# Experts' rows turned by transposing DMAs instead of by TensorE, in a transformer block with a mixture of experts

## Chip, cores, metric

The kernel runs on one core of a Trainium2 chip. The metric is the device time of the whole program in microseconds (us), the median of several runs. Engines: TensorE (PE: matrix products and, in this kernel, transposes), VectorE (DVE), ScalarE (ACT), GpSimd (POOL), and SyncE (SP), which issues most of the DMAs. An instruction waits on semaphores, and each engine works through its own instructions in order.

## What is computed

One block over 4096 tokens of width 256: attention with 16 heads, residual and layer norm, then a mixture of 8 experts of which each token uses two, residual and layer norm. The part that matters here is the mixture:

```
probs = softmax(x @ Wg);  topv, topi = top_k(probs, 2)
pos   = position of the token among those of its expert;  keep = pos < cap      # cap = 1076
buf[expert * cap + pos] = x                                                      # each kept token, twice
h = gelu(buf[e] @ W1[e] + b1[e])          # 1076 x 256 by 256 x 1024, for each of 8 experts
y = h @ W2[e] + b2[e]                     # 1076 x 1024 by 1024 x 256
out[token] += gate * keep * y[slot of token]
x = layernorm(x + out)
```

## The kernel before

**Stages.** Attention fills the first 780 us or so, with the router of the earlier token blocks woven in. Then the router's last block runs (class `Last`), then the eight experts one after the other (function `experts`), then the last layer norm (class `Combine`). The change touches the experts.

**Where the rows come from.** The router's GpSimd scatters write each kept token as a row of 260 floats (1040 bytes) into `slots_x` in memory, row `expert * 1076 + position`. The first 1024 bytes are the token's 256 values as bf16, high part, and 256 as bf16, low part. The last four floats are tags, from which VectorE makes the token's number (`entry`) and gate (`weight`).

**Tiles of an expert.** `CAP` is 1076 rows, `ST` = 9 tiles of 128 rows, the last with `LAST` = 52. `SB` = [(0, 3), (3, 6), (6, 9)] groups the tiles into three sub-blocks of 384, 384 and 308 columns. `HC` = 8 is the hidden width in units of 128. Everything that an expert loads has two buffers, `u` = 0 and 1, so expert e + 1 is prepared during expert e.

**Loads.** SP's `load(u, e)` (L2338 to L2342) reads the rows with tags into `xe` in three DMAs: tiles 0 to 2 (semaphore `x_first`), tiles 3 to 7 and tile 8 (`x_loaded`). Before the loop it waits, in `last.sync`, for all the router's scatters, then issues `load(0, 0)` and `load(1, 1)`. In the loop it waits (L2351 to L2353) until expert e's weights are split, its rows transposed (`x_mm`) and its entries made, and then issues the weights of e + 2 (two DMAs of 1024 KB) and `load(u, e + 2)`. These waits end shortly after expert e has begun.

**Turning the rows.** The first product needs tokens along the free axis, with the 256 input values across partitions. TensorE's `transpose` (L2404) makes four 128x128 bf16 transposes of a tile into PSUM (`ps_x`). ScalarE's `tokens` (L2474) copies them into `xs`. For expert 0, tiles 0 to 2 are turned before its first product and tiles 3 to 8 between its first products. For each later expert e + 1, tile k is turned right before tile k of expert e's `down`.

**Order on TensorE, per expert** (function `one`): 8 `up` products of sub-block 0 and 8 of sub-block 1 (L2416, each six matmuls, hidden chunk q = 0 to 15), `down` of tiles 0 to 2 (L2435, 24 matmuls a tile), 8 `up` of sub-block 2 (q = 16 to 23), `down` of tiles 3 to 5 and 6 to 8. An `up` of chunk q needs ScalarE to be done with chunk q - 4 (PSUM `ps_h` has 4 buffers). `down` of tile k needs VectorE to have read tile k - 2 (`y_sum`, `ps_y` has 2 buffers).

**Order on ScalarE**: gelu of each chunk (L2483, `hidden`), which needs VectorE to be done with chunk q - 4 of `hid`; behind q = 5 and q = 13 the next expert's `W1` and `W2` are rounded to bf16 (L2263, `weights_high`); behind q = 15 the copies `tokens` of tiles 0 to 2, behind q = 23 those of tiles 3 to 8.

**Order on VectorE**: `entries` (the tags, L2559 to L2567), then `split` of chunks 0 to 15 (two operations, L2535 and L2537), then `out` of tiles 0 and 1, `split` of chunks 16 to 23, `out` of tiles 2 to 8. An `out` adds the bias out of PSUM into `yb` (L2521, after which TensorE may reuse that buffer) and multiplies by the gate into `y` (L2526). `y` has three buffers, so `y` of tile k waits until the scatter of tile k - 3 has landed (`y_stored`).

**Order on GpSimd**: the low part of the next `W1` (`w1s`, L2269), the scatters of tiles 0 to 2 (L2372, adding rows of `y` into `result`), the low part of the next `W2` (`w2s`), the scatters of tiles 3 to 8.

## Time and profile before

| | |
|---|---|
| runs, median (lowest to highest) | 1235.44 us (1235.28 to 1236.4), 3 runs |
| profiled execution, span | 1233.1 us; 2.3 us of the median lie outside the span |
| busy in the span | PE 94%, ACT 74%, DVE 52%, POOL 29% |
| experts | from 820.62 (first `up`) to 1197.45 (last `down`), 376.8 us |
| one expert | 47.2 us for those that prepare the next one, 44.4 us for the last |
| last layer norm and stores | from 1197.45 to 1233.1 |

A row of the timeline gives start and duration in us, the engine (PE matmuls, PEld weight loads that overlap them, SPq what SP's queue issues), the line of the program, the operation with output and inputs, a count, and in square brackets how long the engine had been idle and what ended that. Times are from the start of the span. DMA shares are of 16 engines.

### The profile page before, as it was taken

What the parts mean: (1) busy time and instruction counts of PE and PEld (TensorE: products, weight loads), DVE (VectorE), ACT (ScalarE), POOL (GpSimd) and SP (SyncE); (2) the same over time, 40 slices, a digit from 0 to 9 for tenths busy, and PEclk for the clock granted to TensorE, in tenths of its full rate; (3) what the DMA queues carried; (4) which work ended last, traced back from release to release, by engine and by line L of the source; (5) the groups of instructions that cost most, each with busy time, mean ns of one, the idle gap of its engine ahead of it and who ended that gap; (6) DMA issues with size and microseconds to landing.
All of it is one profiled execution on the core that took longest, in us unless ns stands there. A gap on an engine that the chain in (4) does not pass through costs nothing. (4 is left out here: it accounts for less than half of the span.)

```text
span 1233.1 us, 24778 instructions
## 1 busy us (share of the span) xinstructions
PE 1160.2 (94%) x8880; PEld 511.0 (41%) x8880; DVE 635.4 (52%) x1802; ACT 907.5 (74%) x1181; POOL 352.1 (29%) x391
## 2 busy tenths in 40 slices
PE   9999999999999999999999989699999999999980
PEld 4332222222222222222222111277777787787770
DVE  5644343132366345724353203548767767767747
ACT  3889999999999999999999989344434435435314
POOL 5521111111123112232222220033453453552440
PEclk9999999999999999999999999799999999999995
DMA  6842421332321331214120101543443523430226
GB/s 186 178 112 79 96 66 61 80 89 73 80 77 51 112 87 45 78 55 106 40 78 27 47 14 26 180 139 86 115 72 84 129 30 106 124 34 11 28 23 272
DMA packets 84099, 104.10 MB, mean 84 GB/s; under 512 B 15415, under 2 KB 69308, under 8 KB 83984
## 3 DMA queue, kind: packets, MB, share of 16 engines
q1 hardware_dynamic: 66520, 76.80, 21.9%
q0 software_dynamic: 15968, 24.12, 9.3%
q10 hardware_dynamic: 1496, 1.68, 0.4%
q8 instruction: 68, 1.11, 0.4%
q14 instruction: 47, 0.39, 0.1%
HBM read 56.88 MB, written 47.96 MB: 85 GB/s over the span
## 5 line engine op out<-in xcount | busy, mean ns | idle before, releaser
L1497 ACT ACTIVATE prob<-ps_s 128x1024 f32<-128x1024 f32 (+4 forms) x841 | 709.1, 1006 | 41.8 <-PE ps_s L1380 39.0
L1397 PE MATMUL ps_o<-prob,v_aug 128*17 128x512 f32 (+3 forms) x3236 | 420.3, 568 | 3.0 <-DVE acc L1581 2.3
L1380 PE MATMUL ps_s<-qop,kop 51*128 51x512 f16 (+3 forms) x1618 | 273.1, 370 | 14.9 <-issue 3.9
L1380 PEld LDWEIGHTS ps_s<-qop,kop 51*128 51x128 f16 x1618 | 66.0, 93 | 399.3 <-ACT prob L1497 358.1
L2435 PE MATMUL ps_y<-w2s,hs 128*128 128x256 bf16 (+1 forms) x1728 | 189.1, 273 | 0.6 <-DVE yb L2521 0.6
L2483 ACT ACTIVATE hid<-ps_h,b 128x384 f32<-128x384 f32 (+1 forms) x192 | 105.1, 560 | 108.6 <-PE ps_h L2416 80.8
L2416 PE MATMUL ps_h<-xs,w1s 128*128 128x384 bf16 (+1 forms) x1152 | 179.9, 315 | 5.2 <-ACT hid L2483 4.5
L1581 DVE COPY acc<-ps_o 32x512 f32<-32x512 f32 (+2 forms) x108 | 74.2, 687 | 205.9 <-PE ps_o L1397 204.3
L2435 PEld LDWEIGHTS ps_y<-w2s,hs 128*128 128x128 bf16 (+1 forms) x1728 | 157.7, 99 | 17.5 <-DVE yb L2521 0.7
L2372 POOL DMA_INDIRECT result<-y,entry x72 | 111.6, 1550 | 175.5 <-DVE y L2526 140.6
L1533 POOL TENSOR_SCALAR_AFFINE_SELECT prob<-prob 128x256 f32<-128x256 f32 (+1 forms) x179 | 68.7, 395 | 310.3 <-ACT prob L1497 308.6
L2416 PEld LDWEIGHTS ps_h<-xs,w1s 128*128 128x128 bf16 x1152 | 111.2, 98 | 68.8 <-ACT hid L2483 7.2
L2040 POOL DMA_INDIRECT slots_x<-xsplit,dest_all x64 | 64.0, 1000 | 252.2 <-ACT prob L1497 195.9
L2474 ACT ACTIVATE xs<-ps_x 128x512 bf16<-128x512 bf16 (+1 forms) x72 | 40.0, 570 | 103.8 <-PE ps_x L2404 103.7
L1397 PEld LDWEIGHTS ps_o<-prob,v_aug 128*17 128x17 f32 x3236 | 58.5, 95 | 129.2 <-issue 81.4
L2535 DVE CAST hs<-hid 128x384 bf16<-128x384 f32 (+1 forms) x192 | 92.0, 479 | 38.6 <-ACT hid L2483 38.1
L2537 DVE TENSOR_TENSOR hs<-hid,hs 128x384 bf16<-128x384 f32 (+1 forms) x192 | 102.2, 532 | 6.6
L2526 DVE TENSOR_SCALAR y<-yb,weight 128x256 f32<-128x256 f32 (+1 forms) x72 | 45.7, 635 | 13.1 <-DMA result<-y,entry 8.5
L829 DVE CAST x_all<-ps_r 128x256 f16<-128x256 f32 x24 | 10.2, 424 | 76.6 <-PE ps_r L680 76.6
L2521 DVE TENSOR_TENSOR yb<-ps_y,b 128x256 f32<-128x256 f32 x64 | 27.0, 422 | 43.5 <-PE ps_y L2435 43.1
L2269 POOL TENSOR_TENSOR w1s<-w,w1s 128x2048 bf16<-128x2048 f32 x7 | 28.6, 4083 | 44.5 <-ACT w1s L2263 26.4
L1907 DVE TENSOR_TENSOR slogit<-ps_r,xg 128x8 f32<-128x8 f32 x28 | 4.7, 167 | 68.9 <-PE ps_r L1871 68.9
(206 smaller groups left out, 796.8 us busy)
## 6 DMA issues: line engine op xcount, KB each, us to landing
w<-in_W SPq DMA_DIRECT2D x16, 1024.0 KB, 7.5
slots_x<-empty POOLq DMA_DIRECT2D x12, 520.0 KB, 3.9
qop<-fparts_q SPq DMA_DIRECT2D x42, 128.0 KB, 4.7
xe<-slots_x SPq DMA_DIRECT2D x8, 650.0 KB
aT<-attnT SPq DMA_DIRECT2D x16, 256.0 KB
x_all<-in_x SPq DMA_DIRECT2D x8, 512.0 KB
result<-x_all SPq DMA_DIRECT2D x8, 512.0 KB
x_all<-result SPq DMA_DIRECT2D x8, 512.0 KB, 6.5
```

Source lines behind the costliest of these rows:

```text
L1380: mm = pe.matmul(ps_s[:, u.p % SLOTS_S, e, a.q0:], o.key(e, a.h, a.kt), o.query(e, a.h, a.b, a.q0), start=True, stop=True)
L1397: mm = pe.matmul(ps_o[32 * c:32 * c + VW, a.q0:], o.v[:, a.kt, a.h], prob[:, t % RING, c % 2, c // 2, a.q0:], start=a.first, stop=a.last)
L1497: act.activation(prob[:, t % RING, n, e:z, q0:], ps_s[:, u.p % SLOTS_S, e:z, q0:], ACT.Exp, scale=1.0 / (SCALE * SCALE)).then_inc(exp_done, 1)
L1533: pool.affine_select(own, own, [[0, z - e], [1, P]], ALU.is_ge, 0.0, base=0, channel_multiplier=-1).then_inc(masked, 1)
L1581: dve.tensor_copy(acc[rows, a], ps_o[rows]).then_inc(evicted, 1)
L2040: pool.indirect_dma_start(out=r.slots_x, out_offset=bass.IndirectOffsetOnAxis(ap=r.dest_all[:, n, m:m + 1], axis=0), in_=r.xsplit[:, m // ...
L2372: pool.indirect_dma_start(out=result, out_offset=bass.IndirectOffsetOnAxis(ap=entry[0:n, u, k:k + 1], axis=0), in_=y[0:n, k % 3], in_offse ...
L2416: mm = pe.matmul(ps_h[:, q % 4, 0:w], w1s[:, u, i1, c, m * P:(m + 1) * P], xs[:, u, i2, c, a:a + w], start=(t == 0 and c == 0), stop=(t == ...
L2435: mm = pe.matmul(ps_y[to:to + n, (ST * u + k) % 2, 0:D], hs[:, (3 * u + sbk) % 2, i1, m, o:o + n], w2s[:, u, i2, m, :], start=(t == 0 and ...
L2483: act.activation(hid[:, q % 4, 0:w], ps_h[:, q % 4, 0:w], ACT.Gelu_apprx_tanh, bias=b1[:, e, q % HC:q % HC + 1]).then_inc(gelu, 1)
L2535: dve.tensor_copy(hs[:, sl, 0, q % HC, 0:w], hid[:, q % 4, 0:w]).then_inc(h_high, 1)
L2537: dve.tensor_tensor(hs[:, sl, 1, q % HC, 0:w], hid[:, q % 4, 0:w], hs[:, sl, 0, q % HC, 0:w], ALU.subtract).then_inc(h_low, 1)
```

## The change

The rows are no longer loaded as they lie. `sync` issues, per expert, two DMAs that transpose on their way from `slots_x` into `xs`: rows 0 to 383 and rows 384 to 1087 (`TURNED`; 1076 is rounded up to a multiple of 16, the twelve rows more are never used). Two more DMAs bring the tags alone, 16 bytes a row, into `tags`. `xe`, `ps_x`, TensorE's `transpose`, ScalarE's `tokens` and their semaphores are gone. TensorE waits for the first part before sub-block 0 of `up` and for the second before sub-block 1. ScalarE runs its 24 chunks without a break. As the DMA now writes `xs` itself, SP's loop waits until all of expert e's `up` products are done (`h_mm`) where it waited for its transposes, and only then issues the weights and rows of e + 2. VectorE's entries wait for the tags.

```diff
--- before.py
+++ after.py
@@ -2223,6 +2223,7 @@
 
 
 SB = [(0, 3), (3, 6), (6, ST)]
+TURNED = [(0, 3 * P), (3 * P, -(-CAP // 16) * 16)]
 
 
 class Experts:
@@ -2274,7 +2275,7 @@
     w1s, w2s, b1, b2, ident, ws, ye_mm = X.w1s, X.w2s, X.b1, X.b2, X.ident, X.ws, X.ye_mm
     with ExitStack() as st:
         warm = sb("warm5", [1, 1], F32)
-        xe = sb("xe", [P, 2, ST, ROW], F32)
+        tags = sb("tags5", [P, 2, ST, ROW - D], F32)
         same = sb("same", [P, ST], F32)
         pick = sb("pick", [P, ST], F32)
         weight = sb("weight", [P, 2, ST], F32)
@@ -2287,12 +2288,9 @@
         y_other = sb("y_other", [HALF, D], F32)
         ps_h = psum("ps_h", [P, 4, QB], F32, st)
         ps_y = psum("ps_y5", [P, 2, QB], F32, st)
-        ps_x = psum("ps_x", [P, 2, 2 * QB], BF16, st)
-
-        x_first = [sem(f"xe_first{u}") for u in range(2)]
-        x_loaded = [sem(f"xe_loaded{u}") for u in range(2)]
-        x_mm = sem("x_mm")
-        x_out = sem("x_out")
+
+        x_turned = [[sem(f"x_turned{u}{k}") for k in range(len(TURNED))] for u in range(2)]
+        tags_loaded = [sem(f"tags_loaded{u}") for u in range(2)]
         h_mm = sem("h_mm")
         gelu = sem("gelu")
         h_high = sem("h_high")
@@ -2305,7 +2303,6 @@
         y_stored = [sem(f"y_stored{k}") for k in range(3)]
 
 
-        nc.sync.sem_inc(x_out, 2)
         nc.sync.sem_inc(h_low, 4)
         nc.sync.sem_inc(ye_mm, 2 * ST)
         nc.sync.sem_inc(h_mm, 2 * 24)
@@ -2331,15 +2328,18 @@
             for u in range(2):
                 one(E - 2 + u, E // 2 - 1, u, u == 0)
 
-        xs_d = slots_x[0:SLOTS].rearrange("(e r) d -> e r d", e=E)
+        rows_d = slots_x.bitcast(BF16)
         with nc.Block() as block:
             @block.sync
             def _(sp):
                 def load(u, e):
-                    z = SB[0][1]
-                    sp.dma_start(xe[:, u, 0:z], xs_d[e, 0:z * P].rearrange("(k p) d -> p k d", p=P)).then_inc(x_first[u], 16)
-                    sp.dma_start(xe[:, u, z:ST - 1], xs_d[e, z * P:(ST - 1) * P].rearrange("(k p) d -> p k d", p=P)).then_inc(x_loaded[u], 16)
-                    sp.dma_start(xe[0:LAST, u, ST - 1], xs_d[e, (ST - 1) * P:CAP]).then_inc(x_loaded[u], 16)
+                    for k, (a, z) in enumerate(TURNED):
+                        sp.dma_start_transpose(xs[:, u, :, :, a:z].rearrange("p a c n -> p (a c) n"),
+                                               rows_d[bass.ds(e * CAP + a, z - a), 0:2 * D]).then_inc(x_turned[u][k], 16)
+                    z = (ST - 1) * P
+                    sp.dma_start(tags[:, u, 0:ST - 1], slots_x[bass.ds(e * CAP, z), D:].rearrange("(k p) d -> p k d", p=P)
+                                 ).then_inc(tags_loaded[u], 16)
+                    sp.dma_start(tags[0:LAST, u, ST - 1], slots_x[bass.ds(e * CAP + z, LAST), D:]).then_inc(tags_loaded[u], 16)
 
                 last.sync(sp, X, io)
                 load(0, 0)
@@ -2348,7 +2348,7 @@
                     for u in range(2):
                         e = 2 * i + u
                         sp.wait_ge(ws, e * 2 + 2)
-                        sp.wait_ge(x_mm, e * ST + ST)
+                        sp.wait_ge(h_mm, e * 24 + 24 + 48)
                         sp.wait_ge(entry_done, e * 4 + 4)
                         X.load_weights(sp, io, u, e + 2)
                         load(u, e + 2)
@@ -2390,20 +2390,6 @@
             def _(pe):
                 last.tensor(pe, ps_h, ps_y[:, 0], ps_y[:, 1])
                 pe.wait_ge(X.const, 16 * (E + 3))
-
-                def transpose(e, i, u, k):
-                    if k == 0:
-                        pe.wait_ge(x_first[u], i * 16 + 16)
-                    if k == SB[0][1]:
-                        pe.wait_ge(x_loaded[u], i * 32 + 32)
-                    pe.wait_ge(x_out, e * ST + (k + 1))
-                    alone(pe)
-                    n = rows_of(k)
-                    rows = xe[0:n, u, k, 0:D].bitcast(BF16)
-                    for c in range(4):
-                        mm = pe.transpose(ps_x[:, (ST * u + k) % 2, c * P:c * P + n], rows[:, c * P:(c + 1) * P],
-                                          ident[0:n, 0:n])
-                    mm.then_inc(x_mm, 1)
 
                 def up(e, u, sbk, m):
                     w = width(sbk)
@@ -2417,11 +2403,8 @@
                                            start=(t == 0 and c == 0), stop=(t == 2 and c == 1))
                     mm.then_inc(h_mm, 1)
 
-                def down(e, i, u, sbk, ahead):
+                def down(e, u, sbk):
                     for k in range(*SB[sbk]):
-                        if ahead:
-
-                            transpose(e + 1, i + u, 1 - u, k)
                         n = rows_of(k)
                         o = (k - SB[sbk][0]) * P
                         pe.wait_ge(y_sum, e * ST + (k + 1))
@@ -2438,25 +2421,18 @@
 
                 def one(e, i, u, ahead):
                     pe.wait_ge(ws, e * 2 + 2)
-                    first = isinstance(e, int) and e == 0
-
-                    pe.wait_ge(x_out, e * ST + (SB[0][1] if first else ST) + 2)
+                    pe.wait_ge(x_turned[u][0], i * 16 + 16)
                     for m in range(HC):
                         up(e, u, 0, m)
-                        if first and SB[0][1] + m < ST:
-                            transpose(0, 0, 0, SB[0][1] + m)
-                    if first:
-                        pe.wait_ge(x_out, ST + 2)
+                    pe.wait_ge(x_turned[u][1], i * 16 + 16)
                     for m in range(HC):
                         up(e, u, 1, m)
-                    down(e, i, u, 0, ahead)
+                    down(e, u, 0)
                     for m in range(HC):
                         up(e, u, 2, m)
-                    down(e, i, u, 1, ahead)
-                    down(e, i, u, 2, ahead)
-
-                for k in range(*SB[0]):
-                    transpose(0, 0, 0, k)
+                    down(e, u, 1)
+                    down(e, u, 2)
+
                 over_experts(pe, one)
 
             @block.scalar
@@ -2464,15 +2440,6 @@
                 last.scalar(act, X)
                 act.wait_ge(X.const, 16 * (E + 3))
                 act.activation(warm[:], b1[0:1, 0, 0:1], ACT.Gelu_apprx_tanh)
-
-                def tokens(e, u, k):
-                    act.wait_ge(x_mm, e * ST + (k + 1))
-
-                    act.wait_ge(h_mm, e * 24 + 24)
-                    n = rows_of(k)
-                    src = ps_x[:, (ST * u + k) % 2, 0:4 * P].rearrange("p (c n) -> p c n", c=4)
-                    act.activation(xs[:, u, :, :, k * P:k * P + n].rearrange("p a c n -> p (a c) n"), src[:, :, 0:n],
-                                   ACT.Identity).then_inc(x_out, 1)
 
                 def one(e, i, u, ahead):
                     def hidden(q):
@@ -2483,24 +2450,11 @@
                         act.activation(hid[:, q % 4, 0:w], ps_h[:, q % 4, 0:w], ACT.Gelu_apprx_tanh,
                                        bias=b1[:, e, q % HC:q % HC + 1]).then_inc(gelu, 1)
 
-                    first = isinstance(e, int) and e == 0
-                    for q in range(2 * HC):
+                    for q in range(3 * HC):
                         hidden(q)
-                        if first and SB[0][1] + q < ST:
-                            tokens(0, 0, SB[0][1] + q)
                         if ahead and q in (5, 13):
                             X.weights_high(act, e + 1, i + u, 1 - u, q // HC)
-                    if ahead:
-                        for k in range(*SB[0]):
-                            tokens(e + 1, 1 - u, k)
-                    for q in range(2 * HC, 3 * HC):
-                        hidden(q)
-                    if ahead:
-                        for k in range(SB[1][0], ST):
-                            tokens(e + 1, 1 - u, k)
-
-                for k in range(*SB[0]):
-                    tokens(0, 0, k)
+
                 over_experts(act, one)
                 z.scalar(act)
 
@@ -2543,8 +2497,7 @@
 
                 def entries(e, i, u):
 
-                    dve.wait_ge(x_first[u], i * 16 + 16)
-                    dve.wait_ge(x_loaded[u], i * 32 + 32)
+                    dve.wait_ge(tags_loaded[u], i * 32 + 32)
                     if not (isinstance(e, int) and e < 2):
 
                         for k in range(3):
@@ -2556,15 +2509,15 @@
                     parts = [(P, slice(0, ST - 1)), (LAST, slice(ST - 1, ST))]
                     for n, ks in parts:
                         mine = X.expert[0:n, bass.ds(e, 1), ks].rearrange("p o k -> p (o k)")
-                        dve.tensor_tensor(same[0:n, ks], xe[0:n, u, ks, D + 1], mine, ALU.is_equal).then_inc(picked, 1)
-                        dve.tensor_scalar(entry[0:n, u, ks], xe[0:n, u, ks, D], 0.5, None, ALU.mult).then_inc(entry_done, 1)
+                        dve.tensor_tensor(same[0:n, ks], tags[0:n, u, ks, 1], mine, ALU.is_equal).then_inc(picked, 1)
+                        dve.tensor_scalar(entry[0:n, u, ks], tags[0:n, u, ks, 0], 0.5, None, ALU.mult).then_inc(entry_done, 1)
                     for q, (n, ks) in enumerate(parts):
                         dve.wait_ge(picked, e * 4 + (q + 1))
-                        dve.scalar_tensor_tensor(out=pick[0:n, ks], in0=same[0:n, ks], scalar=2.0, in1=xe[0:n, u, ks, D + 3],
+                        dve.scalar_tensor_tensor(out=pick[0:n, ks], in0=same[0:n, ks], scalar=2.0, in1=tags[0:n, u, ks, 3],
                                                  op0=ALU.mult, op1=ALU.add).then_inc(picked, 1)
                     for q, (n, ks) in enumerate(parts):
                         dve.wait_ge(picked, e * 4 + (q + 3))
-                        dve.tensor_tensor(weight[0:n, u, ks], pick[0:n, ks], xe[0:n, u, ks, D + 2], ALU.min).then_inc(entry_done, 1)
+                        dve.tensor_tensor(weight[0:n, u, ks], pick[0:n, ks], tags[0:n, u, ks, 2], ALU.min).then_inc(entry_done, 1)
 
                 def one(e, i, u, ahead):
                     entries(e, i, u)
```

## Rows read from the trace of the kernel before

**Rows 1.** Busy time by stage: the fourth expert and the last.
```profile
964.17:1011.41 47.24, 46.53 (x397) 35.87 (x398) 34.29 (x76) 21.29 (x35) 22.01 (x12) 1.00 0.40 91
1153.06:1197.45 44.39, 44.37 (x361) 33.95 (x360) 28.74 (x76) 13.42 (x24) 14.20 (x10) 1.00 0.21 24
```

**Rows 2.** Chain that ended last, fourth expert: start, duration, work.
```profile
989.29 6.28 PE ps_h L2416 x48
995.57 0.22 PE ps_x L2404 x4
```

**Rows 3.** Timeline, from the router's last block to the first expert.
```profile
799.39 19.11 PE L2099 MATMUL ps_y<-aT 128*128 128x256 f32 x80
...
813.98 0.37 SPq L2340 DMA_DIRECT2D xe<-slots_x  x1
...
819.46 0.17 DVE L2559 TENSOR_TENSOR same<-xe,expert_no 128x8 f32<-128x8 f32 x1 [2.12 <-issue]
...
820.62 1.14 PE L2416 MATMUL ps_h<-xs,w1s 128*128 128x384 bf16 x6 [0.73 <-issue]
```

**Rows 4.** Loads of rows (L2340), and SP's queue from 813 to 820.
```profile
DMA to landing us min/median/max: 3.1/8.2/9.5
...
q1 hardware_dynamic: 1619, 1.62, 74.6%
```

**Rows 5.** Timeline, first expert: GpSimd's split, a cast, tiles 0 and 2.
```profile
830.68 4.08 POOL L2269 TENSOR_TENSOR w1s<-w,w1s 128x2048 bf16<-128x2048 f32 x1 [18.02 <-issue]
...
831.01 3.97 DVE L2535 CAST hs<-hid 128x384 bf16<-128x384 f32 x1 [1.55 <-ACT hid L2483]
...
843.25 0.42 DVE L2521 TENSOR_TENSOR yb<-ps_y,b 128x256 f32<-128x256 f32 x1
...
844.19 2.02 PE L2435 MATMUL ps_y<-w2s,hs 128*128 128x256 bf16 x17
```

**Rows 6.** Timeline, fourth expert: entries, yb of tile 0, tile 2 on TensorE.
```profile
966.20 0.17 DVE L2559 TENSOR_TENSOR same<-xe,expert_no 128x8 f32<-128x8 f32 x1
...
985.66 0.42 DVE L2521 TENSOR_TENSOR yb<-ps_y,b 128x256 f32<-128x256 f32 x1
...
986.28 0.39 PE L2404 MATMUL ps_x<-ident,xe 128*128 128x128 bf16 x4
...
986.50 2.78 PE L2435 MATMUL ps_y<-w2s,hs 128*128 128x256 bf16 x24
```

**Rows 7.** Waits of TensorE, fourth expert: total, times, longest.
```profile
PE ps_h L2416 <- ACT hid L2483: 0.7, 1, 0.7
```

**Rows 8.** Timeline, sixth expert: scatters and y of its later tiles.
```profile
1093.34 1.55 POOL L2372 DMA_INDIRECT result<-y,entry  x1 [7.75 <-DVE y L2526]
1093.49 0.35 DVE L2526 TENSOR_SCALAR y<-yb,weight 128x256 f32<-128x256 f32 x1
...
1099.17 1.55 POOL L2372 DMA_INDIRECT result<-y,entry  x1 [0.17 <-issue]
...
1102.88 1.55 POOL L2372 DMA_INDIRECT result<-y,entry  x1 [0.30 <-issue]
1102.92 0.35 DVE L2526 TENSOR_SCALAR y<-yb,weight 128x256 f32<-128x256 f32 x1 [0.93 <-DMA result<-y,entry]
...
1107.46 0.34 DVE L2526 TENSOR_SCALAR y<-yb,weight 52x256 f32<-52x256 f32 x1
```

**Rows 9.** Timeline, first expert: scatter 2, y of tile 3, scatter 3.
```profile
856.36 1.57 POOL L2372 DMA_INDIRECT result<-y,entry  x1 [7.90 <-DVE y L2526]
856.67 5.52 DVE L2526 TENSOR_SCALAR y<-yb,weight 128x256 f32<-128x256 f32 x1
...
863.03 1.55 POOL L2372 DMA_INDIRECT result<-y,entry  x1 [1.00 <-DVE y L2526]
```

**Rows 10.** DMA queues, 966 to 976: GpSimd's while SP's loads.
```profile
q0 software_dynamic: 262, 0.21, 17.1%
```

**Rows 11.** Busy time and granted clock after the last product.
```profile
1202.00:1204.00 2.00, 0.00 (x0) 0.00 (x0) 0.00 (x0) 0.00 (x0) 0.00 (x0) 0.50 0.14 8
```

## Prediction, made before the changed kernel ran

> **What bounds the kernel now.** Busy time by stage first: an expert that prepares the next one takes 47.24 us with TensorE busy for 46.53 of them at a granted clock of 1.00 (the third number from the right), the last one, which prepares nothing, 44.39 us [rows 1]. So TensorE sets the pace, and the 2.85 us between the two are what preparing costs it. The chain of waits then says what these are: before a tile's 24 matmuls the chain holds 0.22 us of transposes [rows 2], nine times an expert, so 2.0 us; and TensorE's waits show one of 0.7 us on ScalarE's gelu among the first products [rows 7]. Behind that wait stands VectorE: gelu needs a buffer that VectorE has split.
>
> That second finding decides the sum, so I followed VectorE through one expert, in the timeline. From its entries to `yb` of tile 0 are 19.46 us without a gap worth naming (966.20 to 985.66): 16 splits of about 0.9 and one cast that a GpSimd split beside it holds up, as the cast at 831.01 is held for 3.97 us beside the split that began at 830.68 [rows 5, 6]. TensorE's tile 2 needs that `yb`. It ends at 986.08, the transposes of tile 2 begin at 986.28: VectorE is 0.2 us ahead, no more. At the end of the expert the gate is another one: `y` of tile 8 needs scatter 5 landed. A scatter lands 3.75 us after its start (1099.17 to the `y` of tile 6 that waited for it, 1102.92), others of this kind up to 3.9; I take 3.85. Scatter 5 starts at 1102.88, lands at 1106.73, and `y` of tile 8 starts at 1107.46 [rows 8]: 0.73 to spare, call it 0.8. So a second loop runs just under TensorE's: entries, splits, tile 2, the third sub-block's splits, `y` of tile 2, scatter 2, GpSimd's split of `W2`, scatters 3 to 5, `y` of tile 8, entries. Of the 2.0 us only tile 2's transposes lie in it.
>
> **Steady state, experts 1 to 5.** TensorE alone would gain 2.0 us. In the second loop two things give way. Tile 2: without the transposes of tiles 0 and 1 TensorE would be there at 986.28 - 0.44 = 985.84, but `yb` ends at 986.08; with 0.08 for the semaphore its matmuls start at 986.16 instead of 986.50 [rows 6], 0.34 earlier. At the end, the slack of 0.8 before scatter 5 is used up. From there the loop is as long as it was: 0.34 + 0.78 = 1.12 us an expert, and TensorE's wait of 0.7 grows by the other 0.9.
>
> ScalarE's nine copies an expert go too; ScalarE is busy for 21.29 of 47.24 us [rows 1] and appears nowhere in the loop but with a gelu, so nothing follows. SP's wait moves. It ended shortly after an expert's start; now it ends with the last `up`, at 995.57 (989.29 + 6.28 [rows 2]), 31.4 us after the expert's start at 964.17. Queued behind it are 2 MB of weights, the transposing DMAs and the tags. The weights are first read by ScalarE some 8 us into the next expert (GpSimd's part follows at 830.68, 10 us after 820.62 [rows 3, 5]), so they have about 23 us; at the rate below they need 7. The turned rows are wanted 63 us after the wait ends. Both are covered; were the cover gone, each missing us would cost one.
>
> But that traffic now lies beside scatters 2 to 8, on whose landing the loop depends. While SP's queue was full, GpSimd's queue took 17.1% of 16 engines over 10 us for 262 packets, 0.10 us a packet [rows 10]; a scatter has 8 per engine. If each waits for nothing, the cost is 0; if each waits for one packet of equal length, 0.8 us. Most of the transfers should be over when scatter 5 starts, 44 us in, so I take 0.2: 0.92 us an expert, 5 x 0.92 = 4.6 us.
>
> **Expert 6 and the last.** Expert 7 has no split of weights beside it, waits for nothing, 44.37 of 44.39 us busy [rows 1], and follows TensorE. So expert 6 gives tile 2's 0.34, and its tiles 3 to 8 give 6 x 0.22 = 1.3 in full: 1.6 us. The stage behind, norm and stores, is not touched.
>
> **The start.** This is where the new operation is on the path, and no row shows one. The load was issued at 813.98 and its first 390 KB had landed 3.1 us later [rows 3, 4]. In those microseconds 1619 packets with 1.62 MB took 74.6% of 16 engines x 7 us = 83.6 us [rows 4]: 52 ns for a packet of 1 KB, 19.4 GB/s an engine, 310 GB/s in all. So 390 KB are 1.26 us of transfer and 1.8 are fixed; data flows from 815.8. A row must be cut into at least four pieces of 256 bytes, since its 512 values go to four groups of 128 partitions. Call the time of a piece on its engine t. The first part (384 rows) has 96 pieces an engine, both parts (1088 rows) 272. From below: t = 13 ns, as fast as bytes were copied. From above: t = 52 ns, a piece as dear as a whole packet of 1 KB. I take the middle, 26 ns, a rate of 157 GB/s, as pieces of a quarter of the size should lie between.
> First part: 815.8 + 2.5 = 818.3. TensorE runs its filling matmuls until 818.50 [rows 3], so it begins at 818.6, 2.0 us sooner than at 820.62, and without transposes between its products. Second part: 822.9, wanted at 826.5. Tags: 67 pieces an engine more, 1.7 us, at 824.6. That is the one that counts: VectorE's entries began at 819.46 [rows 3] and now begin at 824.6, and 19.5 us later comes `yb` of tile 0, at 844.1 instead of 843.25. TensorE's eight buffers run full meanwhile and its lead is gone; tile 2 starts at 844.1 + 0.42 + 0.08 = 844.6 instead of 844.19 [rows 5]: 0.4 us lost.
> Ends: at 13 ns the tags are there at about 819.7, VectorE is never late and TensorE's earlier start carries through, 2.5 us gained; at 52 ns they are there at 815.8 + 14.1 + 3.5 = 833.4, 9.2 us lost.
>
> Expert 0 has something of its own. Its `y` of tile 3 began 0.31 us after scatter 2 and was held for 5.52 us, so that scatter 3 began at 863.03 [rows 9]; in the sixth expert it began 0.15 us after scatter 2, took 0.35 us, and scatter 3 followed 5.83 us after scatter 2 instead of 6.67 [rows 8, 9]. Without the transposes of tile 3 `y` comes 0.22 sooner against scatter 2, on the good side: 0.84 us. Expert 0 in the loop: -0.4 + 0.84 + 0.78 = 1.2 us.
>
> **Sum.** 1.2 + 4.6 + 1.6 = 7.4 us. The profiled execution would span 1233.1 - 7.4 = 1225.7; with the 2.3 us that the median lies above the span, 1228.0.
>
> **The Trainium skill on the price of a piece.** Rows 4 give 52 ns for a plain packet and say nothing of a turned one. The skill speaks on both sides. "VectorE: DVE Perf Modes", section "The three transpose paths", gives 1309 ns for a 128x128 bf16 block by DMA and 390 ns on TensorE; its section "Rules for kernel authors" names TensorE first where PSUM will do as destination. Taken as a rate, which is an estimate of mine, that is 34 blocks x 1.309 = 44.5 us an expert; the result is the second rival below, at about 1267. "Advanced Engine Details and Errata", section "X-Bar Transpose (TRN2)", calls transposing DMAs as fast as regular ones; by that the start would be at my lower end and the time 1225. No run so far bears out either.
>
> **Rivals.**
> *Full gain.* VectorE's loop has more give than I read, and TensorE gets its 2.0 us: 7 experts x 2.0, 1.3 of expert 0's own transposes, less or more by the start (-2 to +2): about 15, so 1220. For it: TensorE is busy for all but 0.7 us. Against it: the 0.2 and 0.8 us of slack above. 0.10.
> *Slow turning (slower).* Turning costs several times a copy. Place: the start of expert 0. At t = 104 ns, what an adding packet takes in rows 10, both parts land at 815.8 + 28.3 and the tags 7 us later, at 851. TensorE then stands from 818.5 to 826 and again for the second part; after the last product the clock stood at 0.50, the 1.2 GHz level, from 1202 [rows 1, 11], so this adds a little. The entries are 26.5 us later than in my case: 1228.0 + 26.5 = 1254. It decides from the point where the 7.4 us are eaten: tags at 832, t near 47 ns, inside my bounds. Later experts stay covered, 35 us of transfer against 63. 0.22.
> *Crowded scatters.* The turning DMAs hold engines in long stretches and scatters 3 to 5 land L us later; each of seven experts pays L. At L = 1.1 nothing but the ends is left, 1233; at L = 2, 1240. For it: the loop has no slack left. Against it: the price per packet in rows 10, and transfers that should mostly be over. 0.10.
> *Forecast*, t from 13 to 47 ns: 0.58.
>
> **Range and chances.** The forecast's own range is 1224 (t = 13, no crowding: 2.9 + 1.1 less) to 1235. With full gain below and the nearer half of the slow cases above: 1221.5 to 1242; left out are most of slow turning beyond 75 ns (0.13) and the lower tail of full gain (0.04). About 0.2%, 2.5 us, is what a measurement can tell. Faster by more: the forecast but its dearest t (0.54), full gain (0.10), a little crowding (0.02), 0.66. Within: 0.09. Slower: slow turning beyond t = 55 and crowding with L over 1.5, 0.25.
>
> **What would show it.** In the new trace: the first `up` at 818.6 and the entries of expert 0 near 824.6 (time of landing, hence t); experts 1 to 5 at 46.3 us; TensorE's wait for gelu at 1.3 to 1.7 us an expert and a wait of `y` of tile 8 on the scatter; expert 7 unchanged at 44.4. I am wrong if the entries come after 832, if experts fall to 45.3 (full gain), or if scatters land more than 5 us after their start.

## Result and profile after

| | before | changed |
|---|---|---|
| median (lowest to highest) | 1235.65 us (1235.28 to 1236.4), 4 runs | 1224.26 us (1222.37 to 1226.66), 4 runs |
| ratio to before, 95% interval | | 0.9908 (0.9894 to 0.9922) |
| profiled span | 1233.1 | 1220.3 |
| first load of rows issued | 813.98 | 812.49 |
| from there to the last product | 383.5 | 372.3 |
| expert 0 | 49.2 | 45.3 |
| one expert, 1 to 5 | 47.1 to 47.3 | 45.8 to 46.8 |
| expert 6, expert 7 | 47.1, 44.4 | 45.4, 44.4 |

The changed kernel is 11.4 us faster in the median and 11.2 us faster by the stage that the change touches. 1.5 us of the 12.8 by which the two spans differ lie ahead of the first load, in code that no kernel here changes; over the thirteen profiles of this study that load is issued anywhere from 810.2 to 815.3. So what is compared below is the stage, from the first load of rows to the last product, and the median stands beside it. Of its 11.2 us, 1.5 lie between the first load and the first `up`, 3.9 in expert 0, 4.2 in experts 1 to 5 and 1.6 in expert 6. Expert 0 was longer before than the 47.2 us that the text ahead of the prediction gives for every expert that prepares the next one, since TensorE also turned six tiles of its own rows in it:

```profile
820.62:869.77 49.15, 48.12 (x420) 37.05 (x421) 34.59 (x64) 23.95 (x41) 18.77 (x9) 1.00 0.35 88
```

Busy time by stage of the changed kernel, for experts 0, 3, 6 and 7 (columns as in rows 1: PE, PEld, DVE, ACT, POOL, then granted clock, DMA share, GB/s); experts 3 and 7 answer to [rows 1]:

```profile
817.66:862.96 45.30, 44.71 (x361) 33.84 (x360) 31.14 (x69) 16.49 (x26) 17.59 (x8) 1.00 0.60 112
955.86:1002.35 46.49, 44.71 (x362) 33.84 (x360) 34.48 (x77) 16.50 (x26) 22.07 (x11) 1.00 0.47 95
1094.86:1140.30 45.44, 44.73 (x363) 33.86 (x361) 34.62 (x77) 16.49 (x26) 22.22 (x11) 1.00 0.23 26
1140.30:1184.74 44.44, 44.44 (x362) 34.01 (x360) 28.42 (x77) 13.44 (x24) 15.74 (x10) 1.00 0.22 26
```

TensorE's busy time in expert 3 fell from 46.53 to 44.71; the transposes are what is gone. The expert shortened by only 0.75, and the rest is a longer wait of TensorE for gelu, where [rows 7] has 0.7:

```profile
PE ps_h L2402 <- ACT hid L2450: 1.7, 1, 1.7
```

Expert 6, during which nothing is loaded, is at 45.44, 1.6 us shorter than before.

The start, timeline of the changed kernel (answers to [rows 3, 5]):

```profile
812.49 4.44 SPq L2337 DMA_TRANSPOSE xs<-slots_x  x2
...
817.66 13.81 PE L2402 MATMUL ps_h<-xs,w1s 128*128 128x384 bf16 x84
...
820.31 0.17 DVE L2512 TENSOR_TENSOR same<-tags,expert_no 128x8 f32<-128x8 f32 x1 [4.46 <-DMA tags<-slots_x]
...
826.38 4.07 POOL L2270 TENSOR_TENSOR w1s<-w,w1s 128x2048 bf16<-128x2048 f32 x1 [15.21 <-issue]
...
838.95 0.42 DVE L2475 TENSOR_TENSOR yb<-ps_y,b 128x256 f32<-128x256 f32 x1
```

And SP's queue from 812.5 to 820.5 (packets, MB, share of 16 engines; answers to [rows 4]):

```profile
q1 hardware_dynamic: 6270, 1.32, 84.4%
```

84.4% of 16 engines over 8 us are 108 us for 6270 packets, 17 ns each. That is a mean over unlike packets: taken apart by size, the 5093 turned pieces of 256 bytes took 19 ns each (18 in the median) and the 1076 of 16 bytes, the tags, 9 ns. The entries of expert 0 begin 7.8 us after the load is issued (820.31 - 812.49). `yb` of tile 0 comes 26.5 us after it; before it was 29.3 (843.25 - 813.98 [rows 3, 5]).

The end of expert 3, same kernel: scatters 2 to 5, and `y` of tiles 5 to 8 (answers to [rows 8]):

```profile
988.17 0.38 SPq L2256 DMA_DIRECT2D w<-in_W  x1
...
989.21 10.04 SPq L2337 DMA_TRANSPOSE xs<-slots_x  x2
...
991.06 1.55 POOL L2372 DMA_INDIRECT result<-y,entry  x1 [7.38 <-DVE y L2480]
...
996.88 1.55 POOL L2372 DMA_INDIRECT result<-y,entry  x1 [0.17 <-issue]
998.44 0.35 DVE L2480 TENSOR_SCALAR y<-yb,weight 128x256 f32<-128x256 f32 x1 [1.24 <-DMA result<-y,entry]
...
998.73 1.55 POOL L2372 DMA_INDIRECT result<-y,entry  x1 [0.31 <-issue]
...
1000.59 1.55 POOL L2372 DMA_INDIRECT result<-y,entry  x1 [0.30 <-issue]
...
1001.97 0.35 DVE L2480 TENSOR_SCALAR y<-yb,weight 128x256 f32<-128x256 f32 x1 [2.84 <-DMA result<-y,entry]
...
1003.88 0.44 DVE L2480 TENSOR_SCALAR y<-yb,weight 128x256 f32<-128x256 f32 x1 [1.22 <-DMA result<-y,entry]
...
1005.13 0.48 DVE L2473 TENSOR_TENSOR yb<-yb,y_other 52x256 f32<-52x256 f32 x1
...
1005.64 0.65 DVE L2480 TENSOR_SCALAR y<-yb,weight 52x256 f32<-52x256 f32 x1
```

A `y` that waited for its scatter dates the landing. Scatter 2 lands 7.4 us after its start (998.44 - 991.06), scatters 3 and 4 after 5.1 (1001.97 - 996.88, 1003.88 - 998.73), where [rows 8] had 3.75. `y` of tile 8 follows VectorE's own work on `yb` (1005.13 to 1005.61) without idle time, so it didn't wait for scatter 5; nor does it in experts 0 to 5 of this run. What holds VectorE up are scatters 2, 3 and 4: 1.24, 2.84 and 1.22 us. The weights are issued at 988.17, the turning DMAs from 989.21 to 999.25.

### The profile page after: what moved, and what is told of

It reads as the page before. It is cut to its first block and busy times, and to the rows that moved or that the text cites. A ratio compares the mean times of both kernels' runs of the same rounds, so it can differ in the third digit from the quotient of the medians.

```text
span 1220.3 us, 23933 instructions
## 1 busy us (share of the span) xinstructions
PE 1144.6 (94%) x8592; PEld 494.8 (41%) x8592; DVE 634.3 (52%) x1802; ACT 869.8 (71%) x1109; POOL 352.7 (29%) x391
## 5 line engine op out<-in xcount | busy, mean ns | idle before, releaser
L2418 PE MATMUL ps_y<-w2s,hs 128*128 128x256 bf16 (+1 forms) x1728 | 182.7, 273 | 0.5 <-DVE yb L2475 0.2
L2491 DVE TENSOR_TENSOR hs<-hid,hs 128x384 bf16<-128x384 f32 (+1 forms) x192 | 117.3, 611 | 6.6
L2489 DVE CAST hs<-hid 128x384 bf16<-128x384 f32 (+1 forms) x192 | 77.9, 406 | 26.9 <-ACT hid L2450 26.6
L2480 DVE TENSOR_SCALAR y<-yb,weight 128x256 f32<-128x256 f32 (+1 forms) x72 | 46.9, 651 | 37.2 <-DMA result<-y,entry 33.6
L680 PE MATMUL ps_r<-xs_half,ws_half 128*128 128x256 f16 x288 | 39.8, 274 | 0.0
```

The lines of the kernel that those rows point to most:

```text
L2418: mm = pe.matmul(ps_y[to:to + n, (ST * u + k) % 2, 0:D], hs[:, (3 * u + sbk) % 2, i1, m, o:o + n], w2s[:, u, i2, m, :], start=(t == 0 and ...
L2489: dve.tensor_copy(hs[:, sl, 0, q % HC, 0:w], hid[:, q % 4, 0:w]).then_inc(h_high, 1)
L2491: dve.tensor_tensor(hs[:, sl, 1, q % HC, 0:w], hid[:, q % 4, 0:w], hs[:, sl, 0, q % HC, 0:w], ALU.subtract).then_inc(h_low, 1)
```

## Experiments

For each, the stage from the first load to the last product, experts 1 to 5 and the median; each median has its own runs of before beside it.

| run | stage | experts 1 to 5 | expert 6 | median | ratio (95%) |
|---|---|---|---|---|---|
| before | 383.5 | 47.1 to 47.3 | 47.1 | | |
| changed | 372.3 | 46.3, 46.6, 46.5, 46.8, 45.8 | 45.4 | 1224.26 | 0.9908 (0.9894 to 0.9922) |
| moved_only | 384.2 | 47.1 to 47.3 | 47.1 | 1235.34 | 0.9993 (0.9981 to 1.0005) |
| w_early | 368.8 | 45.4 to 46.1 | 45.4 | 1219.99 | 0.9869 (0.9846 to 0.9892) |
| rows_late | 368.3 | 45.4 to 45.7 | 45.4 | 1222.65 | 0.9894 (0.9866 to 0.9923) |
| y9_after | 368.1 | 45.4 to 45.6 | 45.4 | 1217.66 | 0.9852 (0.9833 to 0.9870) |
| plain_copy | 375.5 | 47.1, 47.2, 47.1, 47.1, 45.8 | 45.8 | 1227.47 | 0.9937 (0.9919 to 0.9955) |
| tags_mid | 378.5 | 47.2, 48.2, 48.1, 48.1, 45.6 | 46.5 | 1230.79 | 0.9959 (0.9942 to 0.9975) |
| twice | 389.8 | 48.0, 50.5, 49.1, 49.2, 47.0 | 46.7 | 1242.14 | 1.0057 (1.0037 to 1.0077) |
| all_three | 368.4 | 45.4 to 45.7 | 45.4 | 1219.45 | 0.9871 (0.9853 to 0.9889) |
| tags_early | 370.5 | 45.9, 46.1, 45.7, 46.3, 45.6 | 45.5 | 1221.64 | 0.9888 (0.9866 to 0.9910) |
| copies_kept | 372.4 | 45.9, 46.5, 46.4, 46.9, 45.8 | 45.4 | 1223.23 | 0.9902 (0.9884 to 0.9919) |
| pe_kept | 392.6 | 47.1, 48.1, 53.2, 48.9, 50.4 | 47.9 | 1239.18 | 1.0026 (1.0016 to 1.0036) |

**The moved load alone** (moved_only): the kernel before, with one wait more.

```diff
                         sp.wait_ge(x_mm, e * ST + ST)
+                        sp.wait_ge(h_mm, e * 24 + 24 + 48)
                         sp.wait_ge(entry_done, e * 4 + 4)
```

> The kernel before, whose SP queue waits, as the changed kernel does, for the last up product of expert e before it issues the weights and rows of e + 2; the rows are still turned by TensorE. My theory (a loop over VectorE, GpSimd and scatters 3 to 5 with 0.8 us of slack): scatter 3 lands late beside the load, scatter 5 hardly; experts 1 to 5 between 47.2 and 47.7 us, in all 0 to 2.5 us slower than before. Rival (the moved load delays the loop strongly, and the changed kernel gains in spite of it): the y of tile 6 waits 3 to 4 us and hands on at least 1 us to each of the experts 1 to 6, 6 us or more slower in all.

VectorE waited 3.7 us in expert 3 for scatters instead of 1.4, and nothing followed: the experts have their old lengths, and the 0.7 us by which the stage is longer lie ahead of the first product. So the crowding, scatters that land late beside SP's load, is there, and the kernel before had slack for it. In the changed kernel that slack is used up.

**Away from the scatters, in two steps.** w_early takes the weights out of the way:

```diff
                         sp.wait_ge(ws, e * 2 + 2)
-                        sp.wait_ge(h_mm, e * 24 + 24 + 48)
                         sp.wait_ge(entry_done, e * 4 + 4)
                         X.load_weights(sp, io, u, e + 2)
+                        sp.wait_ge(h_mm, e * 24 + 24 + 48)
                         load(u, e + 2)
```

> The changed kernel, with the weights of e + 2 issued shortly after expert e begins, as before the change; only the transposing DMAs and the tags wait for the last up product. My theory: 1.1 MB less than 40 us into the expert, so scatter 3 lands in about 4 us instead of 7, y of tile 6 waits 1 us; each of the experts 1 to 6 gains 0.1 to 0.4 us, 1 to 2 us in all against the changed kernel. Rival (turning itself, not the weights, holds up the scatters): landing stays near 7 us and the time within 0.5 us of the changed kernel's.

rows_late is the same with `e * 24 + 24 + 48 + 1` in the lower wait.

> As the one with early weights, and the transposing DMAs wait besides for the first up product of expert e + 1, so that nothing at all lies beside the scatters 3 to 5. My theory: scatters land in 3.8 to 4 us, experts 1 to 5 at 46.1 us, 1.5 to 2.5 us faster than the changed kernel. Rival (crowding costs nothing, since only the last scatter counts): within 0.5 us of it.

Expert 3 of w_early and of rows_late, busy time by stage:

```profile
953.76:999.89 46.13, 44.72 (x363) 33.82 (x361) 34.93 (x76) 16.48 (x26) 22.06 (x11) 1.00 0.47 95
```

```profile
956.28:1001.93 45.65, 44.73 (x363) 33.85 (x361) 34.28 (x76) 16.50 (x26) 22.35 (x11) 1.00 0.49 96
```

The stage gains 3.5 and 3.9 us on the changed kernel, more than the 1 to 2 and 1.5 to 2.5 that my theory gave. With the weights gone, `y` of tile 5 no longer waits for scatter 2 in any expert, with the turning DMAs where they were; so the rival of w_early, that turning itself holds the scatters up, falls. (What the expectations of w_early and tags_early call scatter 3 is scatter 2 as counted here.) The experts of rows_late come to 45.6, not to the 46.1 at which I had put the second loop (the one over VectorE and the scatters). That loop was wrong by a term, and the timeline shows which. In my prediction VectorE has no gap from its entries to `yb` of tile 0. It has one, where gelu stands behind ScalarE's rounding of `W1`. Below, the operation that GpSimd's split holds up, in the fourth expert of before, of rows_late and of the changed kernel:

```profile
973.30 3.97 DVE L2535 CAST hs<-hid 128x384 bf16<-128x384 f32 x1 [0.88 <-ACT hid L2483]
```

```profile
965.48 3.97 DVE L2489 CAST hs<-hid 128x384 bf16<-128x384 f32 x1 [0.41 <-ACT hid L2450]
```

```profile
965.25 4.36 DVE L2491 TENSOR_TENSOR hs<-hid,hs 128x384 bf16<-128x384 f32 x1
```

There are 0.88 us of idle time before the held cast, then 0.41, then none; in the changed kernel the cast is already done, and the operation behind it is the one that is held. Entries that begin late use this gap up before they cost anything.

**No wait on the scatters of the same expert** (y9_after): nine buffers for `y`. The edit, without the two lines that follow from it (the scatter reads and VectorE writes `y[0:n, k]`):

```diff
-        y = sb("y", [P, 3, D], F32)
+        y = sb("y", [P, ST, D], F32)
-                    if not (isinstance(e, int) and e == 0 and k < 3):
-                        dve.wait_ge(y_stored[k % 3], e * (16 * ST // 3) + (k // 3) * 16)
+                    if k == 0 and not (isinstance(e, int) and e == 0):
+                        for v in range(3):
+                            dve.wait_ge(y_stored[v], e * (16 * ST // 3))
```

> The changed kernel with nine buffers of y, one for each tile, so that no y waits for a scatter of the same expert. My theory (the loop through scatter 5 holds experts 1 to 5 at 46.3 us, above TensorE's 45.4): the experts fall to 45.4 to 45.8, 3 to 5 us faster than the changed kernel, about 1220; TensorE's wait for gelu falls back to 0.5 to 0.8 an expert. Rival (VectorE's own work from entries to tile 0 sets the pace, scatters don't): experts stay at 46.2 to 46.6, within 0.5 us of the changed kernel.

```profile
951.63:997.21 45.58, 44.72 (x362) 33.84 (x361) 34.66 (x76) 16.48 (x26) 22.12 (x11) 1.00 0.47 96
```

The stage takes 368.1 us, 4.2 less, with all traffic where the change put it. TensorE's wait for gelu is back to what it was before:

```profile
PE ps_h L2402 <- ACT hid L2450: 0.7, 1, 0.7
```

So it is the wait of `y` for its scatter that hands the crowding on. The median, 1217.66, is the lowest of all, 6.6 us below the changed kernel's; by the profiles 2.3 of these are an earlier start of the stage (810.17 against 812.49), not its doing. rows_late shows the opposite: the stage is as short, but in the profile it began at 814.64, and the median is only 1.6 us lower.

**What the crowding is made of.** plain_copy brings the same 256-byte pieces without turning them. The edit in `load` (its range of rows and TensorE's four times higher waits are left out here):

```diff
-                        sp.dma_start_transpose(xs[:, u, :, :, a:z]..., rows_d[bass.ds(e * CAP + a, z - a), 0:2 * D])
+                        for c in range(4):
+                            sp.dma_start(xs[:, u, c // 2, c % 2, a:z].rearrange("p (k j) -> p k j", j=P),
+                                         rows_d[bass.ds(e * CAP + a, z - a), c * P:(c + 1) * P].rearrange("(k p) j -> p k j", p=P))
```

> The changed kernel with each transposing DMA replaced by four plain ones that bring the same rows in the same 256-byte pieces and don't turn them (output wrong: the first products see unturned rows; 1152 rows instead of 1088, 6% more). My theory (a turned piece costs about what a plain piece of 256 bytes costs): expert 0's tags land within 1 us of where the changed kernel has them, y waits for scatters as long, time within 1.5 us of it. Rival (turning is what fills the DMA engines): tags 1.5 us or more sooner, scatters land sooner, experts 1 to 4 below 46.0 us.

```profile
960.60:1007.68 47.08, 44.89 (x363) 33.76 (x361) 35.00 (x78) 16.50 (x26) 22.06 (x11) 1.00 0.48 95
```

Plain pieces crowd no less than turned ones; the stage is even 3.2 us longer than the changed kernel's, to which 6% more rows and eight DMAs in place of two may contribute. How much is theirs is open. The entries of expert 0 began 8.8 us after the load, against 7.8. So turning is not what fills the engines. My bound of 1.5 us was missed, on the side against the rival.

twice issues each turning DMA once more, first into a buffer of its own (`twice[:, u, :, a:z]`), with TensorE's waits raised to 32.

> The changed kernel with each transposing DMA issued twice, the first time into a buffer that nobody reads. My theory (17 ns a piece): the tags of expert 0 land 4.5 to 5 us later, which costs the start about 4.5 us; and 1.1 MB more beside the scatters, so that experts 1 to 4 rise from 46.5 to 47 to 48 us; about 1232. Rival (the crowding comes from the weights' 2 MB alone): the start as above, experts within 0.2 us, about 1229.

```profile
815.18 1.57 SPq L2338 DMA_TRANSPOSE twice<-slots_x  x1
...
827.89 0.17 DVE L2515 TENSOR_TENSOR same<-tags,expert_no 128x8 f32<-128x8 f32 x1 [9.36 <-DMA tags<-slots_x]
```

Entries begin 12.7 us after the load is issued instead of 7.8: 272 pieces an engine more cost 4.9 us, 18 ns each. `yb` of tile 0 comes 30.9 us after it instead of 26.5, 4.4 later; experts 1 to 5 rise to between 47.0 and 50.5. The stage is 17.5 us longer, more than twice what I had expected. Scatter 4 now lands 7.3 to 7.7 us after its start in experts 1 to 3, by the `y` of tile 7 that waited for it. About 1.7 us of expert 2's 50.5 are another thing (my estimate from the row below): for 3.4 us behind a wait of 2.1 us for gelu, the granted clock of TensorE stood at 0.50, the 1.2 GHz level.

```profile
935.30:938.60 3.30, 3.30 (x11) 1.55 (x12) 3.19 (x8) 2.46 (x5) 0.00 (x0) 0.50 0.03 7
```

tags_mid moves the two tag DMAs between the two turning ones; tags_early takes them out of `load` and issues them as soon as the entries of expert e are made:

```diff
+                        sp.wait_ge(entry_done, e * 4 + 4)
+                        load_tags(u, e + 2)
                         sp.wait_ge(ws, e * 2 + 2)
                         sp.wait_ge(h_mm, e * 24 + 24 + 48)
-                        sp.wait_ge(entry_done, e * 4 + 4)
```

> The changed kernel with the two tag DMAs issued between the first and the second transposing DMA. My theory (VectorE's entries wait for the tags at the start): entries of expert 0 begin about 5 us after the load is issued instead of 7.8, its splits wait for the first gelu only, yb of its tile 0 comes 0.8 to 1.3 us sooner after the load; experts 1 to 6 as in the changed kernel; about 1 us faster. Rival (GpSimd's split, not the tags, sets that yb): no change in it.

> The changed kernel, with the tags of e + 2 loaded as soon as expert e's entries are made, early in expert e; weights and transposing DMAs as in the changed kernel. Theory after the run with the tags in the middle (the 1076 packets of 16 bytes a load are what scatter 3 lands behind): experts 1 to 4 fall from 46.3-46.8 to 45.5-46.0 us, from the first load of rows to the last product 369 to 370 us instead of 372.3. Rival (weights and turned rows fill the engines, the tags only add a little): experts 1 to 4 stay above 46.2, 371.5 us or more.

Entries of expert 0 in tags_mid, and expert 3 of both:

```profile
814.58 1.57 SPq L2338 DMA_TRANSPOSE xs<-slots_x  x1
...
819.65 0.17 DVE L2515 TENSOR_TENSOR same<-tags,expert_no 128x8 f32<-128x8 f32 x1 [1.70 <-DMA tags<-slots_x]
```

```profile
960.48:1008.53 48.05, 45.02 (x362) 33.60 (x360) 34.57 (x76) 16.50 (x26) 22.10 (x11) 1.00 0.46 91
```

```profile
955.81:1001.55 45.74, 44.72 (x363) 33.83 (x361) 34.27 (x77) 16.49 (x26) 22.31 (x11) 1.00 0.48 96
```

At the start the rival holds: entries come 5.1 us after the load instead of 7.8, and `yb` of tile 0 still 26.5 after it. GpSimd's split of `W1` begins 13.9 us after the load in both kernels. In the steady state tags_mid was the surprise: its stage is 6.3 us longer, and this pointed at the tags. Their 1076 packets of 16 bytes, moved ahead of the longer turning DMA, are enough to push experts 2 to 4 to 48 us; by what path an order of issue does this is not shown. With the tags out of the way altogether the stage is 1.8 us shorter, between the theory (2.3 to 3.3) and the rival (under 0.8), and neither bound holds. The shares don't add up: without the weights beside the scatters 3.5 us come back (w_early), without the tags 1.8, and 4.2 is all that there is (y9_after).

**The two removed parts.** copies_kept leaves ScalarE nine copies an expert, of a constant into a buffer of their own, behind q = 15 and q = 23.

> The changed kernel, with ScalarE doing nine copies of 128x512 an expert as before (of a constant, into a buffer that nobody reads), at the places where it copied the turned rows. Theory (ScalarE had no part in the gain): from the first load of rows to the last product 372 to 373 us, as the changed kernel. Rival (they held up the gelus of the third sub-block): experts 46.9 or more, over 375 us.

The stage is 372.4 us against 372.3: the copies of the steady state had no part in the gain. pe_kept leaves TensorE its four transposes a tile, of the identity. The lines added in `down`:

```diff
+                        if ahead:
+                            for c in range(4):
+                                pe.transpose(ps_x[:, c * P:(c + 1) * P], ident[:], ident[:])
```

> The changed kernel, with TensorE doing four transposes ahead of each tile of down as before (of the identity, into a bank that nobody reads), for all experts but the last. Theory (the gain of the steady state is TensorE's 2.0 us less, out of which crowding takes back up to 1): experts 0 to 6 at 47.1 to 47.4 us, from the first load of rows to the last product 379.5 to 381.5 us. Rival (part of the gain came from elsewhere): experts 1 to 6 below 46.9, or under 378 us.

```profile
863.53:910.63 47.10, 46.55 (x398) 36.02 (x397) 32.60 (x73) 16.47 (x26) 21.91 (x11) 1.00 0.41 82
958.75:1011.91 53.16, 48.40 (x398) 36.52 (x397) 37.52 (x86) 16.48 (x26) 25.34 (x13) 0.97 0.44 86
```

Expert 1 is at 47.10, the length of before, with TensorE busy for 46.55 of it. The later ones go far above it, with idle stretches that the changed kernel doesn't have. One is at the head of expert 4:

```profile
1007.60 1.50 PE L2422 MATMUL ps_y<-w2s,hs 128*52 128x256 bf16 x24
...
1011.72 0.17 DVE L2516 TENSOR_TENSOR same<-tags,expert_no 128x8 f32<-128x8 f32 x1 [0.19 <-issue]
...
1011.91 2.42 PE L2403 MATMUL ps_h<-xs,w1s 128*128 128x384 bf16 x7 [2.81 <-issue]
```

TensorE stood for 2.8 us, and the profile shows nothing that released it. The matmuls behind it then came every 0.32 us instead of every 0.16, and the clock says why:

```profile
1011.80:1015.20 3.40, 3.29 (x11) 1.60 (x12) 0.93 (x9) 0.58 (x1) 1.57 (x2) 0.50 0.06 5
974.30:977.60 3.30, 3.30 (x13) 1.56 (x11) 3.16 (x9) 2.39 (x5) 0.00 (x0) 0.50 0.02 5
1076.70:1080.00 3.30, 3.30 (x13) 1.48 (x11) 3.16 (x8) 2.61 (x4) 0.00 (x0) 0.50 0.00 0
```

Three times within the experts, for 3.4 us each, the granted clock stood at 0.50, the 1.2 GHz level; I estimate the loss from this at 1.7 us each, 5 in all. Each time TensorE had been idle shortly before, for 2.8 us or, at 973.65 and 1075.74, for 1.95 us on gelu. What the 2.8 us waited for was not found. One thing in the trace sets this kernel apart. Experts 4 and 5 run the same loop instructions as experts 2 and 3, and for them before and the changed kernel fetch nothing over q8, a queue that carries instructions in pieces of 16 KB. pe_kept fetches nine pieces from 1008.8 to 1110, the first of them as the 2.8 us begin:

```profile
q8 instruction: 9, 0.15, 0.6%
```

That TensorE waited for such a piece is likely by its time and is not shown. So the run answers neither my theory nor its rival. It shows the transposes in one expert alone: expert 1 is 1.7 us longer than the undisturbed 45.4 of y9_after, and 0.8 longer than the changed kernel's, which I read as the transposes covering waits that crowding causes there.

**The three together** (all_three): tags between, weights early and rows late, nine buffers.

> Tags between the two transposing DMAs, weights early and rows late, and nine buffers of y, together. Expected 45.4 to 45.6 us for experts 1 to 6, the start as with the tags in the middle: 7.5 to 9 us faster than the changed kernel, about 1216. If the nine buffers alone take away all that the crowding costs, it is no more than 1.5 us faster than with them alone.

The stage is 368.4 us, as with nine buffers alone: once no `y` waits for its scatter, nothing of the crowding is left to take away. My 7.5 to 9 us were too high; the stage gained 3.9 and the median 4.8. The median is 1.8 us above that of nine buffers alone. In the profiles its stage began 4.7 us later (814.84 against 810.17), which is enough to explain that.

## Why the prediction held, and where it did not

The forecast was 1228.0 with 1221.5 to 1242 and faster at 0.66; measured 1224.26. The direction and the mechanism, TensorE's 2.0 us and a loop over VectorE and the scatters that takes part of them back, are right. The gain was 11.4 and not 7.4. The difference lies in the start: up to the end of expert 0 the forecast had 1.2 us and the profiles have 5.3. Experts 1 to 6 came out (6.2 forecast, 5.9 measured), but for experts 1 to 5 this is luck, since two errors of opposite sign lie in them.

- *Price of a piece*: 26 ns taken from bounds of 13 and 52; measured 19 in the trace and 18 by twice. A packet of tags, priced at 26 as well, took 9. So the entries of expert 0 came 7.8 us after the load, not 10.6. The first `up` began when the filling matmuls ended, as forecast (817.66, which is 1.5 us sooner after the load than before; the forecast had 2.0). By the Trainium skill's "Advanced Engine Details and Errata", section "X-Bar Transpose (TRN2)", turning is as fast as a regular DMA. The trace agrees for plain pieces of the same 256 bytes (21 ns in plain_copy, 18 in the median), not for rows moved whole: the 52 ns for 1 KB of [rows 4] are 13 ns for 256 bytes. The Trainium skill's "VectorE: DVE Perf Modes", section "The three transpose paths", has 1309 ns for a block; read as a rate this is 164 ns a piece, by my estimate, and a stream of 34 blocks showed about a ninth of that. The 1267 that the prediction gives for such a rate is worked out nowhere in it; its second rival is priced at 1254, for 104 ns.
- *The start*: this is the term that was mis-sized. I had 0.4 us lost at tile 2 of expert 0 and 2.5 gained at the lower end; `yb` of tile 0 came 2.8 us sooner. The step that failed is that the tags count. With them 2.8 us sooner (tags_mid) `yb` stayed where it was; only with them 4.9 later (twice) did it come later, by 4.4. What sets it is the operation held up beside GpSimd's split, which follows ScalarE's rounding, the gelus and so TensorE's start. TensorE began 1.5 us sooner after the load, and the transposes between its products with ScalarE's last copy behind them, 1.1 and 0.2 us, are the rest: GpSimd's split began 2.8 us sooner. [rows 3, 5] could have told me: in expert 0 of before, `yb` of tile 0 came 23.8 us after the entries (843.25 - 819.46), not the 19.46 that I took from the fourth expert. The entries had 4 us to spare there. In the changed kernel it is 18.6 us, in twice 18.2.
- *Tile 2*: 0.34 us gained instead of the 0.66 of three tiles' transposes. Right: undisturbed experts are at 45.43 to 45.6, which is 47.1 to 47.2 less 0.34 and six times 0.22.
- *The slack before scatter 5*: 0.8, sized too small, and the gate was another. The gap of 0.9 on gelu in the same loop belongs to the slack. With it the loop could give TensorE all of the 1.64 us, as rows_late and y9_after do. I had expected `y` of tile 8 to wait for scatter 5. In experts 1 to 5 of the changed kernel it never waits; tiles 5, 6 and 7 do, for scatters 2, 3 and 4. Full gain was nearer to the truth than I had it, but for tile 2's 0.3.
- *Crowding*: 0.2 us an expert, sized far too small. A scatter beside the load lands 1.3 to 3.6 us later, where a count of packets gave 0.8 at most. Landings over 5 us were the sign that I had named for being wrong, and in this term I was. Experts 1 to 4 pay 0.9 to 1.2 of the 1.64 for it, expert 5 0.2, expert 6 nothing. That the sum for experts 1 to 5 came out (4.6 forecast, 4.2 measured) is the two errors cancelling, which is luck.
- *Expert 6*: 1.6, measured 1.6. *ScalarE*: nothing in the steady state, and copies_kept measured nothing; at the start its last copy was worth the 0.2 us named above. *The weights' 23 us*: no wait on them.
- *Scatter 3 of expert 0*: right. `y` of tile 3 is no longer held, and scatter 3 follows scatter 2 by 5.84 us (851.61 to 857.45) instead of 6.67.

## What to carry to other kernels

A transposing DMA can take transposes off a busy TensorE at about the price of moving the bytes in 256-byte pieces, if its rows are wanted late. What it writes is the operand itself, so its buffer comes free later than the raw rows' did, and the load moves to another place in the cycle: look at what lands there, since short scatters beside it took up to twice as long. Where such a landing gates a buffer, one more set of buffers (here six tiles of `y`) gave as much as moving the load about (a stage of 368.1 us against 368.8 and 368.3). A chain with "no gap worth naming" must be added up gap by gap; 0.9 us of idle time was half of its slack. And a duration read in one place must be held against the place where it is used: 19.46 us in the fourth expert were 23.8 in the first, and the difference was the slack of the term that I had called decisive.

## Not expected of the hardware

- Turned pieces: 18 to 19 ns for 256 bytes on an engine, 84.4% of the engines' time for 1.32 MB in 8 us; the same pieces unturned were no faster.
- SP's queue is occupied by a turning DMA for 1.4 to 5.8 us (4.4 in the median of 16) where the 24 plain loads of rows before took 0.3 to 2.2 (medians 0.4, 0.8 and 2.1 of the three DMAs of a load).
- 1076 packets of 16 bytes, placed ahead of the turning DMA of 704 rows, cost 0.9 to 1.6 us in each of experts 1 to 4.
- A scatter that lands in 3.8 us alone needed 5.1 to 7.4 beside SP's load in expert 3.
- Behind idle times of TensorE of 1.95 to 2.8 us its granted clock stood at 0.50 for 3.4 us, three times in the run pe_kept and once in the run twice. In tags_mid it stayed at 1.00 behind a wait of 2.1 us for gelu that ended at 928.78. What makes the difference is open.
- The second pass through the loop of experts fetched no instructions over q8 in before and in the changed kernel, and nine pieces of 16 KB in pe_kept.
